# A weight dequantisation spread over the first attention alone, instead of over everything up to the third layer's gate

## The reference

```python
x = x + _L0_xattn_ref(_layernorm(x, axis=-1), ctx_4096, ...)   # 16 heads of 96, keys from context and x
x = x + _L0_ffn_ref(_layernorm(x, axis=-1), ...)               # 1376 wide, ternary weights, truncation to int8
x = x + _L1_xattn_ref(_layernorm(x, axis=-1), ctx_4096)
x = x + _L1_ffn_ref(_layernorm(x, axis=-1), ...)               # 64 experts of rank 8, top 16
x = x + _L2_xattn_ref(_layernorm(x, axis=-1), ctx_4096, ...)
x = x + _L2_ffn_ref(_layernorm(x, axis=-1), ...)               # 3 experts, top 2
x = x + _L3_xattn_ref(_layernorm(x, axis=-1), ctx_4096, ...)
x = x + _L3_ffn_ref(_layernorm(x, axis=-1), L3_ffn_w1, L3_ffn_w2, L3_ffn_w3)
```

```python
absmax = jnp.max(jnp.abs(flat), axis=1, keepdims=True)
idx = jnp.searchsorted(bounds, flat / absmax)
return (NF4_CODE[idx] * absmax).reshape(shape)
```

## Time and profile before

| | |
|---|---|
| median of 3 runs | 1833.43 us (1831.36 to 1834.33) |
| profiled execution | 1829.38 us, of it a span of 1827.6 us from the first instruction to the last |
| busy in the span | TensorE 1475.9 us (81%), VectorE 1129.2 (62%), ScalarE 464.1 (25%), GpSimd 311.6 (17%) |
| first attention with background | about 60 to 690 us |
| first feed-forward layer | about 690 to 945 us |
| layer 1 and attention of layer 2, up to `gate2` | about 945 to 1207 us |
| mean granted clock of TensorE | 0.871 |

### The profile page before, as it was taken

How to read it: one execution, slowest core, us unless ns; L and a number is a source line. 1 busy time by engine, 2 the same in 40 slices (tenths; PEclk the granted TensorE clock), 3 DMA queues, 4 the chain that set the end, 5 groups by cost and what they waited for, 6 DMA issues and landing times.

```text
span 1827.6 us, 19239 instructions
## 1 busy us (share of the span) xinstructions
PE 1475.9 (81%) x6585; PEld 1165.1 (64%) x6585; DVE 1129.2 (62%) x2623; ACT 464.1 (25%) x994; POOL 311.6 (17%) x186
## 2 busy tenths in 40 slices
PE   4549989989899898979837877858997676679998
PEld 3426666667676666757626766747886565468786
DVE  2466667656776666846796757554458588864241
ACT  2213334232342323313222202112212222222020
POOL 2201111011121111202011102113432312012020
PEclk9779999999899989999955689559998878789999
DMA  4341222213222211122101112100111100001011
GB/s 127 121 127 55 72 66 73 76 45 90 60 69 71 79 48 58 53 74 61 35 24 41 41 38 70 44 16 13 55 49 46 35 1 0 1 23 58 12 37 46
DMA packets 99362, 96.43 MB, mean 53 GB/s; under 512 B 13090, under 2 KB 72370, under 8 KB 99266
## 3 DMA queue, kind: packets, MB, share of 16 engines
q1 hardware_dynamic: 98754, 94.35, 17.8%
q0 software_dynamic: 512, 0.85, 0.2%
HBM read 84.34 MB, written 10.82 MB: 52 GB/s over the span
## 4 chain that ended last, share of the span: by engine, by line
PE 32%; DVE 19%; issue 2%; ACT 1%; DVEq 0%; ACTq 0%
PE bank L1643 29%; DVE st L1128 1%; DVE xn L1146 1%; DVE mx L1496 1%; DVE e L1510 1%; DVE nf_y L1587 1%; DVE xT L1107 1%; DVE sm L1508 1%; PE bank L1983 1%; PE bank L1939 1%; DVE e L1499 1%; PE bank L1668 1%; DVE eT L1516 1%; DVE rt L1117 0%; DVE rt L1116 0%
## 5 line engine op out<-in xcount | busy, mean ns | idle before, releaser
L1643 PE MATMUL bank<-xT,slots 128*128 128x512 f32 (+1 forms) x1920 | 466.9, 401 | 8.8 <-DVE xT L1107 6.8
L802 POOL TENSOR_TENSOR slots<-staging,slots 128x1024 fp32r<-128x1024 f32 (+4 forms) x97 | 229.3, 2367 | 1189.0 <-ACT slots L890 1188.9
L1643 PEld LDWEIGHTS bank<-xT,slots 128*128 128x128 f32 (+1 forms) x1920 | 355.6, 186 | 105.3 <-DVE xT L1107 5.4
L1983 PE MATMUL bank<-nf_y,nf_d 128*128 128x512 f32 (+2 forms) x495 | 193.3, 450 | 82.9 <-DVE nf_w L1597 53.5
L1587 DVE TENSOR_SCALAR nf_y<-nf_w 128x512 fp32r<-128x512 f32 (+2 forms) x495 | 225.0, 483 | 19.4 <-PE bank L1983 18.2
L1643 PE MATMUL bank<-slots,h 128*128 128x512 f32 (+1 forms) x728 | 181.6, 409 | 21.0 <-DVE h L1235 14.9
L1983 PEld LDWEIGHTS bank<-nf_y,nf_d 128*128 128x128 f32 (+1 forms) x495 | 97.0, 201 | 137.9 <-DVE nf_y L1587 63.3
L1643 PEld LDWEIGHTS bank<-slots,h 128*128 128x128 f32 (+1 forms) x728 | 142.2, 196 | 58.0 <-DVE h L1235 15.7
L890 ACT ACTIVATE slots<-staging 128x1024 fp32r<-128x1024 f32 (+4 forms) x97 | 98.1, 1018 | 203.4 <-PE bank L1643 184.1
L1107 DVE TENSOR_TENSOR q<-bank,q 96x256 fp32r<-96x256 f32 (+3 forms) x120 | 61.0, 508 | 125.7 <-ACT q L880 125.7
L1201 DVE TENSOR_TENSOR x<-bank,x 128x512 f32<-128x512 f32 x72 | 49.8, 692 | 140.9 <-PE bank L1643 140.7
(11 more groups left out here) (244 smaller groups left out, 1944.1 us busy)
## 6 DMA issues: line engine op xcount, KB each, us to landing
staging<-in_L_wqkT SPq DMA_DIRECT2D x16, 480.0 KB, 3.5
nf_out<-nf_w SPq DMA_DIRECT2D x30, 256.0 KB, 2.1
staging<-nf_out SPq DMA_DIRECT2D x30, 256.0 KB, 2.9
staging<-in_L_woT SPq DMA_DIRECT2D x16, 384.0 KB, 3.5
staging<-in_L_w SPq DMA_DIRECT2D x12, 512.0 KB, 3.9
nf_a<-nf_max SPq DMA_DIRECT2D x40, 128.0 KB, 3.4
nf_r<-nf_rcp SPq DMA_DIRECT2D x40, 128.0 KB, 3.3
nf_w<-in_L_w SPq DMA_DIRECT2D x15, 256.0 KB, 3.4
```

Of the source, the lines that this page charges most:

```text
L802: g.tensor_tensor(lo, split_source(i), hi.bitcast(FP32), ALU.subtract).then_inc(*sig.mark("weight_low", i))
L1643: ins = mm(dst, l_, r_, start=i == 0, stop=i == len(passes) - 1)
L1983: mm(banks[NF_BANK][0:rows, 0:size], nf_d[0:rows, j - 1, 0:rows], nf_y[0:rows, i % STAIR_RING, 0:size], start=j == 1, stop=j == NPART).the ...
```

## The change

The last step in front of which the background must be done is no longer the first `gate2`, but the first `up0`, the first step of the first feed-forward layer. The same jobs, in the same order among themselves and at the same prices, are so spread over the steps from the first `scores0` to the end of the first attention.

```diff
-BACKGROUND_END = "gate2"
+BACKGROUND_END = "up0"
```

## The result

The changed kernel takes 1957.74 us (median of 4 runs, 1953.71 to 1959.52) against 1832.39 us of the kernel before (4 runs): a ratio of 1.068, with a 95% interval of 1.066 to 1.070. It is slower by 125 us. The forecast was slower by 56 us, with a range up to 1928 us: the sign was right, the size was less than half of what was measured, and the time lies outside the range.

A forecast was written before the change was run, and what follows sets the result against it. TensorE was taken to bound the first attention, engine chains the stages from 945 us. Terms 37.5 + 42 + 21 + 13 + 5 - 30 - 32 = +56.5 us gave 1886, forecast 1888 us; own range 1860 to 1912, wider 1840 to 1928.

The forecast's parts named there:

- The sign, and the stage: Whole kernel slower, chance 0.91; first attention, bound by TensorE, loses more than the later stages give back.
- The fourth matmul: Attention: a group's fourth sum waits for its own group's staircase step, behind VectorE's part of the main step; +42 us.
- Moved matmuls: Attention: 163 staircase matmuls move into it at 0.23 us each; +37.5 us.
- Handover and loads: Attention: waits for nf_end to empty the staircase bank, +21 us; late w3 loads on SP's queue, half reaching TensorE, +13.
- Rival 1: Attention: all of the w3 loads' lateness reaches TensorE, 45 us instead of 13, giving 1920 us; chance 0.17.
- The clock: TensorE's granted clock sags where it has gaps, 0.95 in attention before; a fall was priced only between 1015 and 1133 us.
- Rival 2: Behind the feed-forward layer, 1015 to 1133 us: clock falls from 0.81 to about 0.55, +20 us, 1908 us; chance 0.13.
- The maxima: Stretch from 60 to 137 us: maxima run in the first 10.5 units of room, not 15.2; +5 us.
- Feed-forward layer: First feed-forward layer, 690 to 945 us: staircase matmuls, nf_end waits and steps leave it; -30 us.
- Behind it: Second attention, router and experts, third attention, 945 to 1207 us: staircase work leaves the chain; -32 us.
- The sum: Whole kernel: all terms together +56.5 us, 1886 us on the profiled execution, forecast 1888; chance 0.60.
- Rival 3: Attention: VectorE far enough ahead that no added sum waits; -19.5 us, 1814 us; decides under 19.5 us of waits; chance 0.10.

The follow-up runs named there:

- e11_before_two_queues: Kernel before the change, with STAIR_LAG 4, the load issued with step 5 and the broadcasts of the reciprocals issued by GpSimd: 1786.62 us, 0.976.
- e10_after_two_queues: Changed kernel with STAIR_LAG 4, the load issued with step 5 and the broadcasts of the reciprocals issued by GpSimd: 1813.57 us, 0.990 of the kernel before.
- e13_two_queues_only: Changed kernel with only the broadcasts of the reciprocals moved to GpSimd's queue, lag 2 and load step 8 kept: 1927.45 us, 1.053 of the kernel before.
- e9_fill: Changed kernel with six banks plus 354 unused constant matmuls in front of sums expected to wait: 1945.09 us, against 1957.84 for the six-bank control.
- the middle place: Kernel before with BACKGROUND_END at scores1, so the background ends with the first feed-forward layer: 1902.60 us, 1.038; with all three edits 1790.35 us, 0.978.

## Why the prediction was right or wrong

- *The sign, and the stage.* Right: the loss arises in the first attention, where TensorE is the bound, and the later stages give back less.
- *The fourth matmul, +42 us.* Right in mechanism. The waits for nf_y grew by 57 us, of which 9.4 are the first item's load (14.8 against 5.4). Sorted by the product ahead, 26 waits behind `q0` and `k0` are 1.0 us each and 21 behind `o0` 0.55, 38 us together (forecast 42); the other waits stand behind smaller products. Lag 3 takes 45 us of them away, lag 1 makes them at the old density. One point of the reasoning was too narrow: capping the group doesn't help, because the sum follows its step by a fixed number of jobs wherever the steps stand.
- *Moved matmuls, +37.5 us.* Consistent with what is left when waits are removed: from `e11_before_two_queues` to `e10_after_two_queues` the start of the feed-forward layer moves from 668.7 to 734.1 us, 65 us. TensorE's idle time in attention is 17 us larger there, and the clock (0.97 and 0.96) makes an estimated 7; some 40 are left for the matmuls. Not measured alone.
- *Handover and loads, 21 + 13 = +34 us.* Failed in size: +51. At the 1.76 us that an item without a late load waits, the 33 handovers are 58 us (forecast 56), so that term was right. The other 28 us are the late loads, forecast as 13. VectorE's idle time was forecast well (44 us, measured 39), but "half of it" reaches TensorE was wrong: at w3's items 21 us more of VectorE's idle time went with 37 more of TensorE's. The overlooked step is that `nf_end` is queued behind the scaling, which `e13_two_queues_only` shows. Rival 1 had this mechanism too large (45 for 13).
- *The clock.* The largest failure: the sum had no term for it in attention. 553 us at 0.95 lack 28 us of full speed, 733 at 0.90 lack 73; the 45 us between, times TensorE's busy share of 0.80, are about 36 us. Taken stretch by stretch, TensorE was busy at the lower of its two clocks for 45.5 us of attention before and for 115.5 after; half of the 70 between is 35 us. `e9_fill` gives an estimated 28 us of it back. Rival 2 looked for the clock in the wrong stage: between 1155 and 1268 us it stayed at 0.80.
- *The maxima, +5 us.* About +1: their stretch is 7 us shorter, and 8.4 us of TensorE's work moved from it into attention.
- *Feed-forward layer, -30 us.* Right: -28. *Behind it, -32.* -26: six too many; the clock fell there from 0.55 to 0.50 and from 0.60 to 0.53 in the two attentions.
- *The sum.* For attention, idle +93, matmuls 37.5, clock 36 and maxima 1 make 168 of the 174 us. Against the forecast of 56.5, 17 us more idle time (93 against 76), about 36 for the clock, 8 less given back, 4 lost behind `gate2`, 4 less for the maxima and about 7 unexplained lead to 124.4. So two steps failed: the sum had nothing for the clock in attention, and it let only half of the late loads' lateness reach TensorE. Rival 3 fell: added waits were far above 19.5 us.

Open: why w3's items wait in the middle place as long as in the dense one; why the clock stayed at 0.95 with lag 1; and how the remaining 27 us between the two ends with all edits (1813.57 and 1786.62) divide.

## What to carry to other kernels

Background work that several engines pass on in a fixed order needs slack in that order, and the slack is a number of jobs: look at how many of them stand behind one step of the main work, and whether a consumer needs what stands behind its engine's own copy. Don't queue an instruction that frees a resource behind one that waits for a load. Where TensorE is the bound, a gap in it can cost more than its length, since the matmuls behind it may run at half clock; read the clock of the stretch to see whether they do. And when a move of work costs waits, remove the waits before judging the place: lag 4, an earlier load and a second queue gave 2.4% in the old place, more than the place itself moves once they are in (27 us, 1.5%).

## What the runs showed of the hardware

Adding 354 matmuls in front of waits made a kernel 13 us faster: the mean clock in that stretch rose from 0.89 to 0.95, and the same 248 matmuls took 66.6 instead of 73.5 us. In one place the 18 matmuls that followed gaps of 1.35 and 1.93 us took 8.23 us, against 4.59 for the same 18 elsewhere. Not every gap does this: with lag 1 in the old place, waits of 81 us in attention (45.6 and 35.5) left the mean clock at 0.95, as it was with 48 us of them. Issuing the ten broadcasts of the reciprocals of a w3 item took SP 6.16 us; with them on a second queue VectorE's waits for loads in attention fell from 39.1 to 11.0 us (`e13_two_queues_only`).
